# Rounding and splitting the reloaded rows of heads 1 and 2 inside their scores, and the sources of head 2 later in a block, in a graph attention kernel

## What is computed

```python
def gat_layer(x, W, a_s, a_d, b, edge_index, concat):
    h = (x @ W).reshape(n, H, C)
    src, dst = (edge_index[0], edge_index[1])
    alpha_s = jnp.einsum('nhc,hc->nh', h, a_s)
    alpha_d = jnp.einsum('nhc,hc->nh', h, a_d)
    e = jax.nn.leaky_relu(alpha_s[src] + alpha_d[dst], NEG_SLOPE)
    m = jax.ops.segment_max(e, dst, num_segments=n)
    e = jnp.exp(e - m[dst])
    denom = jax.ops.segment_sum(e, dst, num_segments=n)
    alpha = e / (denom[dst] + EPS)
    out = jax.ops.segment_sum(h[src] * alpha[:, :, None], dst, num_segments=n)
    ...
h = jax.nn.elu(gat_layer(x, W1, ...))      # 8 heads of 768
h = gat_layer(h, W2, ...)                  # 1 head of 768
x = _layernorm(x + h)
```

## Time and profile before

| | us |
|---|---|
| median of 3 runs | 658.85 |
| the three runs | 663.57, 658.73, 658.85 |
| the profiled execution | 660.23 |
| its span | 658.4 |
| TensorE busy in the span | 638.7 |
| VectorE busy | 510.9 |
| ScalarE busy | 333.8 |
| GpSimd busy | 210.3 |

### The profile page before, as it was taken

The page is one execution under the profiler, slowest core; times in us unless marked ns, Lnnn a source line. Parts: engine busy times, 40 slices in busy tenths (PEclk is TensorE's granted clock), DMA queues, the critical chain, the costliest instruction groups (busy, mean ns, idle before and its releaser), DMA issues.

```text
span 658.4 us, 9322 instructions
## 1 busy us (share of the span) xinstructions
PE 638.7 (97%) x3437; PEld 549.0 (83%) x3446; DVE 510.9 (78%) x927; ACT 333.8 (51%) x560; POOL 210.3 (32%) x121
## 2 busy tenths in 40 slices
PE   6999999999989999999999999999999999999995
PEld 4765567989878879988899889988998899878984
DVE  8899996798997977485956684677876787889466
ACT  7798972535614644353535444454436344524272
POOL 0000000132553550357124822473156514641130
PEclk9999999999999999999999999999999999999998
DMA  8413421115052520134112320325043403500002
GB/s 310 155 49 96 144 73 49 48 49 192 26 167 89 200 72 1 49 96 144 49 48 83 109 98 24 97 62 154 25 126 116 143 23 119 195 25 1 1 0 97
DMA packets 22173, 59.36 MB, mean 90 GB/s; under 512 B 2544, under 2 KB 2800, under 8 KB 22128
## 3 DMA queue, kind: packets, MB, share of 16 engines
q1 hardware_dynamic: 22128, 58.76, 27.5%
HBM read 54.03 MB, written 4.72 MB: 89 GB/s over the span
## 4 chain that ended last, share of the span: by engine, by line
PE 76%; DVE 19%; ACT 2%; issue 2%; DMA 0%; SPq 0%; DVEq 0%; ACTq 0%
PE O L1182 21%; PE R L1077 9%; PE R L1083 9%; PE R L1080 9%; PE R L1149 5%; PE R L1155 5%; PE R L1152 5%; PE O L1094 4%; DVE ohd L645 2%; DVE junk L681 2%; DVE hl L706 2%; DVE ohs L647 1%; DVE L L752 1%; DVE junk L808 1%; PE R L1099 1%
## 5 line engine op out<-in xcount | busy, mean ns | idle before, releaser
L1011 POOL TENSOR_TENSOR W2l<-Wr,W2h 128x768 fp32r<-128x768 f32 x48 | 98.9, 2067 | 212.6 <-ACT W2h L404 212.6
L1015 POOL TENSOR_TENSOR Pl<-L,Ph 128x512 fp32r<-128x512 f32 x34 | 53.8, 1594 | 174.3 <-ACT Ph L453 174.3
L1077 PE MATMUL R<-W1h,xTh 128*128 128x384 f32 x312 | 106.4, 341 | 0.0
L1080 PE MATMUL R<-W1l,xTh 128*128 128x384 f32 x312 | 105.4, 338 | 0.0
L1083 PE MATMUL R<-W1h,xTl 128*128 128x384 f32 x312 | 105.4, 338 | 0.0
L681 DVE CUSTOM_DVE_ANT_0 junk<-h,abc 128x768 bf16<-128x768 f32 x64 | 64.5, 1007 | 48.2 <-ACT h L416 46.8
L1182 PE MATMUL O<-W2h,gh 128*128 128x256 f32 (+1 forms) x384 | 79.9, 344 | 0.0
L1182 PE MATMUL O<-W2l,gh 128*128 128x256 f32 (+1 forms) x384 | 77.5, 337 | 0.0
L1182 PE MATMUL O<-W2h,gl 128*128 128x256 f32 (+1 forms) x384 | 77.2, 336 | 0.0
L416 ACT COPY h<-R 128x384 f32<-128x384 f32 x62 | 29.5, 478 | 82.3 <-PE R L1083 76.3
L1094 PE MATMUL O<-ohd,ohs 128*128 128x512 bf16 x255 | 61.9, 389 | 8.2 <-DVE ohs L647 5.7
(11 more groups left out here) (172 smaller groups left out, 1158.0 us busy)
## 6 DMA issues: line engine op xcount, KB each, us to landing
Wr<-in_W SPq DMA_DIRECT2D x101, 384.0 KB, 3.2
abc<-in_as SPq DMA_DIRECT2D x9, 384.0 KB, 4.5
abc<-in_ad SPq DMA_DIRECT2D x9, 384.0 KB, 5.9
h_rows<-h SPq DMA_DIRECT2D x8, 384.0 KB, 2.3
hl<-h_rows SPq DMA_DIRECT2D x8, 384.0 KB, 6.1
xin<-in_xT SPq DMA_DIRECT2D x6, 256.0 KB, 6.1
xr<-in_x SPq DMA_DIRECT2D x1, 1536.0 KB, 7.3
out<-res SPq DMA_DIRECT2D x4, 384.0 KB, 2.3
```

Of the source, the lines that this page charges most:

```text
L1011: e.tensor_tensor(W2l[:, m % N2, :], Wr[:, n, :], W2h[:, m % N2, :].bitcast(f32), ALU.subtract).then_inc(s_w2l, 1)
L1015: e.tensor_tensor(Pl[:, t, d0:d1], L[:, t, d0:d1], Ph[:, t, d0:d1].bitcast(f32), ALU.subtract).then_inc(s_Pl, 1)
L1077: e.matmul(bank[:, 0:HALF], xTh[:, f, xs], hi[:, ws], start=f == 0, stop=False)
L1080: e.matmul(bank[:, 0:HALF], xTh[:, f, xs], lo[:, ws], start=False, stop=False)
```

## The change

It moves instructions and adds none.

- ScalarE: `high_h(2, 0)` goes in front of the exponential of tile 3 in the scores of head 2, `high_h(2, 1)` in front of the last rounding of `Ph`. The other two stay behind `high_sums(2)`.
- VectorE, head 1: `low_h(1, 0)` goes ahead of the scores, `low_h(1, 1)` between the sum of the columns and its rest (`sums_P`). Head 2: `low_h(2, 0)` goes to that place in its own `sums_P`.
- TensorE: `sources(2)` leaves its place between C(0,3) and C(0,4) and goes inside C(0,4), in front of its third part.

```diff
@@ scalar_program
                 if h == 2:
                     high_w2(1, 4)
+
+                    def rows_2(u):
+                        if u == 3:
+                            high_w2(1, 5)
+                        if u > 3:
+                            high_h(2, u - 4)
                     scaled_as(2, 24)
-                    scores(2, 2, 0, NT, ring_bank("r2", 2, 0), (gl_value(1, FT - 1), (s_g, 2 * FT)), 8, lambda u: high_w2(1, 5) if u == 3 else None)
+                    scores(2, 2, 0, NT, ring_bank("r2", 2, 0), (gl_value(1, FT - 1), (s_g, 2 * FT)), 8, rows_2)
                     high_sums(2)
-                    for t in range(NT):
+                    for t in range(2, NT):
                         high_h(2, t)
@@ vector_program
-            def sums_P(h):
+            def sums_P(h, between=None):
 
                 e.wait_ge(s_sd, 3 * h + 2)
                 e.scalar_tensor_tensor(
                     out=y2[:, :], in0=y2[:, :], scalar=EPS / 128, in1=rb[:, :], op0=ALU.add, op1=ALU.add).then_inc(s_sd, 1)
+                if between:
+                    between()
                 e.wait_ge(s_dh, h)
@@
                 if h == 1:
+                    low_h(1, 0)
                     scores(1, 1, 0, NT, ring_bank("r1", 1, 0), 6)
-                    sums_P(1)
+                    sums_P(1, lambda: low_h(1, 1))
...
-                    for t in range(NT):
+                    for t in range(2, NT):
                         low_h(1, t)
                     maxima(2, 0, NT, ring_bank("as", 2, 0))
                 if h == 2:
                     scores(2, 2, 0, NT, ring_bank("r1", 2, 0), 9)
-                    sums_P(2)
-                    for t in range(NT):
+                    sums_P(2, lambda: low_h(2, 0))
+                    for t in range(1, NT):
                         low_h(2, t)
@@ tensor_program
-                    stage_C(h - 1, c, between=(lambda h=h: denominators(h)) if c == (FT - 2 if h == H - 1 else FT - 1) else None)
-                    if c == 3 and h == 1:
-                        sources(2, 24)
+                    stage_C(h - 1, c, between=(lambda: sources(2, 24)) if h == 1 and c == 4 else (lambda h=h: denominators(h)) if c == (FT - 2 if h == H - 1 else FT - 1) else None)
```

## The result

The changed kernel takes 664.12 us (median of 15 runs, 661.79 to 667.15); the kernel before, with as many runs, 658.85 (658.28 to 663.57). The ratio is 1.0058, 95% interval 1.0040 to 1.0077: 3.8 us slower. The medians lie further apart, by 5.3, because nine of the 15 runs of the kernel before fall between 658.3 and 658.9 and the other six between 660.2 and 663.6, so that its median is one of the faster nine; the means differ by 4.2. The forecast was 662.3 with a range of 657.8 to 664.2. The profiled execution took 664.17 with a span of 662.4, against 660.23 and 658.4: 4.0 us more.

A forecast was written before the change was run, and what follows sets the result against it. TensorE, busy 97% of the span, was taken as the bound, so changes elsewhere pay only where it waits. The terms -1.0 + 0 + 3.3 + 1.2 = +3.5 us gave 662.3 us (658.85 + 3.5), range 657.8 to 664.2.

The forecast's parts named there:

- What bounds it, and turns of 2.5 us: TensorE bounds; a `low_h` started with a GpSimd subtraction queued costs about 2.5 us instead of 0.88.
- Head 1, VectorE, -1.0: VectorE's queue in head 1 is one `low_h` shorter; reciprocal and A(1,1) come 1.0 us earlier.
- Head 1, the sources: TensorE waits about 0.6 us for source sums inside C(0,4); the move earns nothing beyond the 1.0.
- Head 2, inside the scores, 0: Moved `high_h` and `low_h` inside head 2's scores only reorder the same work: gain 0.
- Head 2, behind the scores, +3.3: Head 3's weight roundings start 1.47 us earlier, two `low_h` take 2.5 each, A(2,1) is 3.3 us later.
- The clock, +1.2: TensorE's gap ahead of A(2,1) lowers its clock, costing 1.2 us, between ends of 0 and 1.7.
- The sum: Whole kernel: -1.0 + 0 + 3.3 + 1.2 = +3.5 us, so a median of 662.3 us.
- the extra turn in head 1: Rival: head 1's fifth W2l comes before the last `low_h(1, 3)`, losing 1.6 us; +5.1, 664.0 us; chance 0.05.
- the full gain: Rival: all three waits of TensorE (sources, A(1,1), A(2,1)) vanish; -2.8, 656.0 us; chance 0.07.
- the free collision: Rival: head 2's collision is absent or single; -1.0 + (0 to 1.6), 657.9 to 659.5 us; chance 0.2.
- the clock that stays at 2.4 GHz: Rival: as forecast, but TensorE's clock does not fall around A(2,1); +2.3, 661.2 us; chance 0.2.
- the clock that stays low through A(2,5): Rival: half rate from A(2,1) to A(2,5) costs +13.8, altogether +16, 675 us; chance 0.03.

The follow-up runs named there:

- sources_old_place: The changed kernel with `sources(2)` back between C(0,3) and C(0,4): 668.28 us, ratio 1.0117 to the kernel before.
- weights_wait: The changed kernel with ScalarE rounding W1 tiles 3 to 5 of head 3 only after head 2's last row split: 659.73 us, ratio 0.9995 to the kernel before.
- row_split_behind: The changed kernel with head 2's first row split back behind the rest of the sum: 663.97 us, ratio 1.0065 to the kernel before.
- one_row_front: The changed kernel with `low_h(1, 1)` back behind the weighted sums: 667.06 us, ratio 1.0104 to the kernel before.
- head2_only: The kernel before with only the head 2 part of the change: 665.24 us, ratio 1.0084 to the kernel before.
- both_wait: The changed kernel with W1 of head 3 (tiles 3 to 5) and head 1's first three W2 tiles waiting for row splits: 659.94 us, ratio 1.0011 to the kernel before.
- recip_twice: The kernel before with a second, unused whole reciprocal in head 2: 664.80 us, ratio 1.0080 to the kernel before.

## Why the prediction was right

- **What bounds it, and turns of 2.5 us**: right. Held operations of 768 columns took 2.4 to 2.5, and the pairs were counted correctly in both heads.
- **Head 1, VectorE, -1.0**: right, -1.01. The reciprocal was forecast for about 192.5 and started at 193.06, 0.55 of it the later anchor.
- **Head 1, the sources**: the wait of about 0.6 was 0.64. That they earn nothing here was right, and that the rest would lose without them too (1.9 us, sources_old_place). What the prediction had not seen is that the new place alone would cost 1.7.
- **Head 2, inside the scores, 0**: right. The last product had to wait 0.27 for ScalarE's exponential and still ended where it would have (63.47 from the anchor; 64.48 before, less 1.0).
- **Head 2, behind the scores, +3.3**: right, -1.01 to +2.30 is 3.31. The cause is shown by weights_wait and row_split_behind.
- **The clock, +1.2**: the direction was right and the size not. In this profile it cost 2.7, more than the upper end of 1.7, which was taken from the earlier trace rows; the clock stayed low for longer than there. The size differs from profile to profile though TensorE stands still for the same time: with waits of 1.1 to 1.2 and 2.8 us it cost 1.4 in one_row_front, 1.5 in head2_only, 1.6 in sources_old_place, 2.3 in row_split_behind and 2.7 here. The forecast had no row for the fall itself and took it from the last head. It also gave no length for how long TensorE must stand still, and single gaps of 2.5, 2.9 and 3.4 us, each in one profile, left the clock at 2.4 GHz. The 15 runs have mean clocks of 0.995 (four, 661.8 to 662.7 us), 0.992 to 0.994 (eight, 662.7 to 664.8) and 0.987 (three, 666.3 to 667.2); how much of that is head 2 and how much the last head the means don't say.
- **The sum**: 3.5 forecast, 3.8 by the ratio, 5.3 between the two medians. The trace's 4.0 also holds -1.55 that the forecast did not have, the slow stretch of the last head, which the profiled execution of before had and this one had not. The forecast had taken it as given in both. The steps that the forecast did name come to 5.0 in this trace, 1.5 more than it gave them, and the 1.5 is the clock. That the trace's 4.0 comes near 3.5 is therefore luck in part. So is it that the median of 664.12 lies inside the range, 0.1 below its end: with the clock at its full price of 1.7 the sum gives 662.9, and the room above that was there for the extra turn in head 1, which did not come.

Of the rivals, the full gain, the free collision and the clock that stays at 2.4 GHz are excluded by the trace, and so is the clock that stays low through A(2,5). The extra turn in head 1 did not come in the changed kernel, but did in two experiments.

## What to carry to other kernels

Idle time of VectorE was free only where GpSimd was idle too: write both timelines beside each other and count, for each VectorE operation with two SBUF inputs, whether a GpSimd subtraction is queued. When an instruction goes forward in one engine's program, look at what stands behind it there and whom that releases; here a rounding of weights that no matmul needed before B(3), some 19 us later, came 1.5 early and cost 3.3. An order that works may rest on a wait of another engine (the 1.02 us ahead of the sources). A wait that holds back work without haste until the crowded stretch is over can be worth more than filling gaps (1.5 us against 1.0 at A(2,1)). And a gain of 1 us in a trace is not yet a gain in the time, as long as a slow stretch elsewhere costs anything from 0 to 4.7 us.

## What the runs showed of the hardware

- GpSimd gets its turn after each VectorE operation, however many of those follow one another: in the 14 profiles no two VectorE operations with two SBUF inputs ran one behind the other inside a single 768 column GpSimd subtraction. A turn costs VectorE 1.6 us (2.48 instead of 0.88), less than the 1.86 that such a subtraction takes alone.
- A turn costs the same in front of an operation of 4 columns: 1.77 us instead of 0.16 (both_wait).
- Operations with an input in PSUM were not held: the maxima took 0.69 beside a W2l (both_wait), the reciprocal its 3.35.
- TensorE's clock fell to 1.2 GHz behind a single gap of 4.1 us (recip_twice), and behind gaps of 1.1 to 1.2 and 2.8 us with one matmul between them (five profiles); single gaps of 2.5, 2.9 and 3.4 us left it at 2.4 GHz in the one profile of each. The same gaps cost between 1.4 and 2.7 us.
- It also fell behind 24 matmuls two columns wide, during which the profile shows TensorE busy, in 11 of the 14 profiles; the loss up to the end of the span was about 1.5, 3.2 or 4.7 us.
